# Edge stages of a two-layer graph network: a chunk of a block holds consecutive edges in place of every fifth one

## What is computed

```
h = (x @ W.T).reshape(n, H, D)
h_src = h[src]
h_dst = h[dst]
alpha = einsum('ehd,hd->eh', h_src, a_src) + einsum('ehd,hd->eh', h_dst, a_dst)
enc = relu(edge_attr @ edge_W.T + edge_b).reshape(-1, H, D)   # first layer only
alpha = alpha + sum(enc * h_dst, axis=-1)                      # first layer only
alpha = where(alpha >= 0, alpha, 0.2 * alpha)
ex = exp(alpha - segment_max(alpha, dst)[dst])
attn = ex / segment_sum(ex, dst)[dst]
out = segment_sum(h_src * attn[..., None], dst)
```

## Time and profile before

| | |
|---|---|
| median of 3 runs | 9298.79 us (9282.61 to 9309.99) |
| the profiled execution, span | 9356.6 us |
| busy in it | PE 6873.4, DVE 4972.5, ACT 2835.6, POOL 5584.7 us |
| gathers of the edge stages (L731) | 3960 in the loops, busy 5158.7 us, mean 1303 ns |
| loop of the first edge stage | about 0.60 to 3.74 ms of the span |
| loop of the second edge stage | about 5.30 to 8.54 ms of the span |

### The profile page before, as it was taken

How to read it: one execution, slowest core, us unless ns; L and a number is a source line. 1 busy time by engine, 2 the same in 40 slices (tenths; PEclk the granted TensorE clock), 3 DMA queues, 4 the chain that set the end, 5 groups by cost and what they waited for, 6 DMA issues and landing times. The chain is left out here.

```text
span 9356.6 us, 165625 instructions
## 1 busy us (share of the span) xinstructions
PE 6873.4 (73%) x32650; PEld 5243.0 (56%) x32650; DVE 4972.5 (53%) x15411; ACT 2835.6 (30%) x5775; POOL 5584.7 (60%) x4384
## 2 busy tenths in 40 slices
PE   0489999999999998259992666666666666664593
PEld 0356666666666665259982555555555555553593
DVE  2257777777777776501113456655665555565114
ACT  0134444444444444012220222222222222221120
POOL 0058888888888887120003488888888888884203
PEclk9989999999999999579995888888888888886797
DMA  1445555555555555445553344444444444446354
GB/s 53 134 108 126 125 126 126 126 126 126 126 126 126 126 125 117 156 148 179 187 180 120 85 115 116 116 114 114 115 116 114 115 114 114 114 116 163 113 183 137
DMA packets 1501411, 1185.58 MB, mean 127 GB/s; under 512 B 1083493, under 2 KB 1244064, under 8 KB 1475344
## 3 DMA queue, kind: packets, MB, share of 16 engines
q1 hardware_dynamic: 901837, 626.32, 24.7%
q0 software_dynamic: 594272, 543.45, 22.7%
q10 hardware_dynamic: 5256, 15.36, 0.5%
HBM read 1041.62 MB, written 137.28 MB: 126 GB/s over the span
## 5 line engine op out<-in xcount | busy, mean ns | idle before, releaser
L731 POOL DMA_INDIRECT e_rows<-sc_table,e_idx x3960 | 5158.7, 1303 | 1211.9 <-issue 1137.1
L790 PE MATMUL e_ps_o<-e_rows,e_pt 116*128 116x256 f32 x7960 | 2149.6, 423 | 483.0 <-ACT e_pt L847 375.5
L790 PEld LDWEIGHTS e_ps_o<-e_rows,e_pt 116*128 116x128 f32 x7960 | 1625.2, 213 | 826.9 <-issue 594.8
L775 PE MATMUL e_ps_s<-e_ident,e_arep 116*128 116x116 f32 x7960 | 1129.2, 293 | 686.7 <-ACT e_arep L841 672.0
L983 DVE CUSTOM_DVE_ANT_1 e_x<-e_ps_s,e_mask 128x580 f32<-128x580 f32 x796 | 955.4, 1200 | 1176.7 <-PE e_ps_s L775 838.9
L775 PEld LDWEIGHTS e_ps_s<-e_ident,e_arep 116*128 116x128 f32 x7960 | 1035.0, 205 | 843.5 <-issue 839.0
L841 ACT COPY e_arep<-e_rows 116x640 f32<-116x640 f32 x798 | 578.3, 725 | 2253.0 <-DMA e_rows<-sc_table,e_idx 1957.7
L771 PE MATMUL e_ps_s<-e_encr,e_bd 128*128 128x464 f32 (+1 forms) x3184 | 956.6, 433 | 63.7 <-issue 32.2
L1513 POOL DMA_INDIRECT c_g<-sc_yb,f_slot_i x147 | 170.7, 1162 | 1361.1 <-PEq L1495 1291.1
L771 PEld LDWEIGHTS e_ps_s<-e_encr,e_bd 128*128 128x128 f32 x3184 | 532.2, 191 | 662.4 <-issue 658.5
L835 ACT ACTIVATE e_encr<-e_ps_e 128x580 f32<-128x580 f32 x798 | 519.8, 651 | 1137.0 <-PE e_ps_e L762 794.6
(11 more groups left out here) (271 smaller groups left out, 6562.7 us busy)
## 6 DMA issues: line engine op xcount, KB each, us to landing
e_dstb<-sc_dstp SPq DMA_DIRECT2D x804, 290.0 KB
x_w<-in_L_ffn_W_dram SPq DMA_DIRECT2D x112, 1024.0 KB
e_rows<-sc_table,e_idx POOLq DMA_INDIRECT x4020
x_w<-in_L_ffn_w_dram SPq DMA_DIRECT2D x60, 1024.0 KB
sc_xb<-r_zero SPq DMA_DIRECT2D x24, 1024.0 KB
x_xin<-sc_xb SPq DMA_DIRECT2D x86, 256.0 KB
sc_yb<-x_y SPq DMA_DIRECT2D x82, 256.0 KB
e_at<-sc_attrp SPq DMA_DIRECT2D x402, 40.8 KB
```

Source lines behind the costliest of these rows:

```text
L731: pool.indirect_dma_start(rows[0:CK, k, j, :], None, dr["table"][:, :], bass.IndirectOffsetOnAxis(idx[0:CK, k, j:j + 1], 0)).then_inc(s_ro ...
L775: mm = nc.tensor.matmul(banked(ps_s)[:, j, :], arep[0:CK, p, j, :, :].rearrange("p t h -> p (t h)"), ident[0:CK, 0:CK], start=not first, s ...
L790: mm = nc.tensor.matmul(ps_o[:, p, 0:D], pt[0:CK, p, j * P:(j + 1) * P], rows[0:CK, k, j, 0:D], start=(j == 0), stop=(j == CH - 1))
```

## The change

Edge e of a block now belongs to chunk e div 116 at place e mod 116: `idx[p, j]` is the source node of edge 116 j + p. The load of `idx` takes single integers, 116 apart in HBM, where it took runs of five. The two tiles that were read with a step of five are read as they lie. No instruction is added, removed or moved on any engine.

```
-                sp.dma_start(idx[0:CK, k, :], dr["srcp"][bass.ds(e, BE)].rearrange("(p j) -> p j", j=CH)).then_inc(s_load[k], 16)
+                with nc.allow_non_contiguous_dma(reason="a chunk holds consecutive edges, one to a partition"):
+                    sp.dma_start(idx[0:CK, k, :], dr["srcp"][bass.ds(e, BE)].rearrange("(j p) -> p j", j=CH)).then_inc(s_load[k], 16)
...
-                cols = at[:, k, :].rearrange("k (p j) -> k j p", j=CH)
+                cols = at[:, k, :].rearrange("k (j p) -> k j p", j=CH)
...
-                return row.rearrange("p (e j) -> p j e", j=CH)
+                return row.rearrange("p (j e) -> p j e", j=CH)
```

## The result

The changed kernel takes 9349.67 us, the median of three runs (9334.59 to 9355.65), beside 9298.79 before. The ratio is 1.0049, with a 95% interval of 1.003 to 1.0068, so it is slower by 51 us between the medians of these few runs, and by 28 to 63 us by the interval. The profiled execution of the changed kernel has a span of 9332.8 us.

A forecast was written before the change was run, and what follows sets the result against it. Both edge stages were taken as bound by POOL's gathers; +40 us in the first, -28 in the second and 0 for the load gave 9311 us on the median, no change that can be told, range 9225 to 9430.

The forecast's parts named there:

- rival 1: First edge stage: L1000 settles 1.29 us into a gather in nearly every block, +145 us, total 9416; chance 0.28.
- What bounds the kernel: Both edge stages: POOL's gathers and its 0.305 us issue gaps set the pace, with PE and DVE beside it.
- PE, first stage: L761 and L762 without the step: 0.23 us less a block, worth 0 to the time.
- DVE: Both edge stages: L983 about 0.39 us shorter in every block, in itself worth 0 to the time.
- Gathers, second stage: L1000 starting 0.39 us earlier cuts the gathers' excess by 0.07 us a block, -28 us; bounds -117 and +50.
- even spread: L1000's start falls evenly over a gather and its gap, costing a mean of 0.156 us a block; chance 0.38.
- Gathers, first stage: L1000 starting 0.39 us earlier raises the gathers' excess from 0.055 to 0.156 us a block, +40 us.
- The load: Load of `idx` as 580 packets holds SP some 1.3 us a block, covered by issue 15.7 us ahead: costs 0.
- What would show it wrong: POOL gaps above 0.3 us, or mean gather moving over 0.02 us in one stage without the other going opposite.

The follow-up runs named there:

- b_again: The kernel before, run again unchanged beside the changed one: 9299.89 us, ratio 0.9998.
- e3_mask: The kernel before with the mask alone read contiguously on DVE, so the sums are of other edges: 9363.11 us, ratio 1.0069.
- a_again: The changed kernel, run again unchanged: 9344.91 us, ratio 1.0048 to the kernel before.
- g_z1_a: The changed kernel with `z` in PSUM in the second layer, all computed: 9275.36 us, ratio 0.9976 to the kernel before.
- g_z1_b: The kernel before with `z` in PSUM in the second layer, all computed: 9239.4 us, ratio 0.9942.

## Why the prediction failed in its mechanism, and where it was right

The forecast was no change that can be told, 9271 to 9327 with the point at 9311 us. Measured were 9349.67, above that and inside the range of 9225 to 9430. The point lay 12 us above the kernel before and the result 51. That the range holds it is in good part luck: it is 205 us wide, one of the two terms of the sum went the other way, and the other came out of other instructions than the one that was costed. The direction is that of rival 1, whose size (9416) the result doesn't have.

- **What bounds the kernel.** Right. Nearly all of POOL's gaps stayed 0.305 us, and 229 us less of PE and 201 less of DVE gave nothing.
- **PE, first stage.** Worth 0 as said, mis-sized: 2 x (299 + 92) = 0.78 us a block were saved where I took 0.23. The Trainium skill, Advanced Engine Details and Errata, SBUF Cachelines, asks for two hits on each 16-byte line and so pointed to the larger gain, though steps of 10 bytes do give two hits on three lines of five; the trace agrees with the larger gain.
- **DVE.** L983 was to fall by 0.39 us to 0.82; it fell by 0.45 to 0.76. In itself worth 0, as said.
- **Gathers, second stage.** This is the step that failed. It took the excess of 0.295 us a block from an execution that was not typical, and held it against an even spread of `lk` alone, halving the difference for whatever else there was. In b_again it is 66.6 / 398 = 0.167, of which `lk` has 36.0 / 398 = 0.090, already less than the even spread of 0.156 that the term moved it to. So there was nothing to win. It also supposed that shifting L1000 forward by 0.39 us would spread its phases. Instead they gathered where they cost: 238 and 227 gathers start under it in place of 115, and 61% and 58% of the starts of `lk` lie more than 0.87 us into a gather, where it was 29% and an even spread would have 45%. Predicted were -28 us, measured +26 and +17 against b_again. Against the execution that the term was worked out from, the stage did fall, by 34 us, and that agreement is worth nothing.
- **Gathers, first stage.** +40 was forecast, and about half, +19 and +20, was measured. I costed L1000 alone, and it brings a third of the 40, +13 us of excess. +18 come from `mask`, -14 from `z`, +7 from `bd`, -9 from `res`, -1 from the rest, and +5 to +8 are waits. The prediction said in passing that other short instructions with two inputs stay where they are; `bd` is one and doesn't, and the instructions with one input had no term at all, though rows for `mask` and `z` were in the trace. In the Trainium skill, Advanced Engine Details and Errata, Mode Summary under VectorE Performance Modes, a mode with two ports needs, beside conditions on the shape, source and destination in SBUF, and such instructions and GpSimd's block each other. L993 at 0.51 us from SBUF to SBUF and 0.82 into PSUM, with no gather held in the second case, agrees with it, and so does the hold of `z` and `mask` by a gather. The section that I had cited, on instructions with two SBUF inputs, named this mode beside them, and tied the wait on descriptors to it; I used half of the sentence.
- **The load.** Nearly right for this kernel: four waits and 9 to 12 us in place of none. But its reason was incomplete. The 15.7 us of cover (which lie two gathers back from 2033.1 and not three to four; the number is right) were read as a fixed property of the early issue. They hang on PE and DVE getting shorter in the same change. Added alone, the load makes the first stage 133 us longer, 0.33 us a block, for which the prediction's price without the cover was 1.3, and the whole kernel 162. The extra packets came as said (+373,056, 1,274,893 in all on the queue).
- **What would show it wrong** did so by one of its two signs: a few gaps over 0.3 us. The other did not: from b_again to the changed kernel the mean gather went up in both stages (1282 to 1289 and 1299 to 1311 ns), by less than the 20 ns that the sign asked for. In the rows that the prediction was made from it is 1.277 and 1.329 us, and against these it rose and fell as forecast, by the same chance as the stage's length.

What stays open: why the shorter mask step brings `lk` and `mask` onto the starts of gathers rather than away from them. The counts show that it does, in e3_mask, the changed kernel and a_again alike (in the first stage the count under `mask` grows to 140 and 150 only where PE's read is changed too); no run moved the phases at will. Why one execution of the same kernel has 220 such gathers in the second stage and another 115 is open too.

## What to carry to other kernels

When one engine paces a stage by its issue, list every instruction of the neighbours that can hold it, and price them by how many of its starts fall under each; a shorter neighbour can come to lie under more. Take those instructions off the shared resource (here `z` into idle PSUM banks, slower for itself, 0.58% faster in all) before shortening anything that isn't the bound. Before costing a term from a profile, hold its span against the median, and where it is off by more than the effect that you look for, find which stage is off; and a cost that is covered only by slack from another part of the same edit is not free if that part is dropped.

## What the runs showed of the hardware

- A gather of 116 rows that starts while a DVE instruction with two SBUF inputs runs is held to 0.128 us before that one's end, and not at all when one of the inputs lies in PSUM (322 gathers in g_z1_a and g_z1_b, 0.0 us in all).
- An instruction with one input from SBUF to SBUF (580 floats in 0.51 us) holds a gather by the same measure, the overlap less 0.128 us, if the gather starts 0.08 us or more behind it (948 of 949), and not if it starts within 0.06 us (0 of 160). With its output in PSUM it takes 0.82 us and holds none of 261.
- The gather holds such an instruction in turn: one that starts 0.54 to 0.80 us into a gather ends 1.52 to 1.56 us behind the gather's start and takes up to 1.01 us. `lk`, with two inputs, never took more than 0.83.
- bf16 columns with a step of ten bytes cost 669 ns for 464, and 370 without one.
- A load of 580 single elements holds the next issue on its queue for about 1 us, in one to two of ten for 2 to 3, where runs of five leave it at 0.34.
